# Normalised rows and the two small stacks of a fused attention and expert kernel, made by GpSimd instead of VectorE

## The reference, cut to what matters

```python
xn = layernorm(x)                                  # no gain, no bias
kv_c = xn @ W_kv;  kv_c = kv_c * rsqrt(mean(kv_c**2) + 1e-6) * g_kv     # 32 columns
q_c  = xn @ W_q                                    # 64 columns
k = concat(kv_c @ W_kdec, rope(xn @ W_krope))      # 16 heads of 8 + 32
q = concat(q_c @ W_qdec,  rope(q_c @ W_qrope));  v = kv_c @ W_vdec
att = softmax(causal(q k^T / sqrt(40))) @ v @ W_o
moe = sum over the top 2 of 8 of w_e * (silu(xn W1_e + b1_e) W2_e + b2_e) + 0.1 * shared(xn)
out = x + att + moe
```

## Time and profile before

| what | us |
|---|---|
| median of 3 runs | 778.36 |
| lowest and highest of them | 774.90, 778.86 |
| the profiled execution | 774.29 |
| its span, first to last instruction | 772.6 |
| busy in the span: TensorE | 650.1 |
| VectorE | 609.2 |
| ScalarE | 391.7 |
| GpSimd | 285.8 |
| mean granted TensorE clock | 0.946 of full |

### The profile page before, as it was taken

How to read it: one execution, slowest core, us unless ns; L and a number is a source line. 1 busy time by engine, 2 the same in 40 slices (tenths; PEclk the granted TensorE clock), 3 DMA queues, 4 the chain that set the end, 5 groups by cost and what they waited for, 6 DMA issues and landing times. The chain is left out here.

```text
span 772.6 us, 14715 instructions
## 1 busy us (share of the span) xinstructions
PE 650.1 (84%) x4646; PEld 510.9 (66%) x4646; DVE 609.2 (79%) x1632; ACT 391.7 (51%) x842; POOL 285.8 (37%) x284
## 2 busy tenths in 40 slices
PE   0557977898887899889798998888789999999995
PEld 0445756667665677667576776665558888888884
DVE  3758898878788878878888778888457777779896
ACT  1212544445453445545355445443357777777772
POOL 3322541626536254463242433233300000257574
PEclk9957999999999899999999999999989999999998
DMA  4254655466566465655444555435844778789753
GB/s 128 83 174 160 195 174 191 147 214 206 187 211 192 138 189 187 192 182 197 129 148 145 150 160 153 148 129 176 275 150 138 244 246 251 262 285 295 238 172 93
DMA packets 66135, 141.66 MB, mean 183 GB/s; under 512 B 9054, under 2 KB 34699, under 8 KB 66059
## 3 DMA queue, kind: packets, MB, share of 16 engines
q1 hardware_dynamic: 61059, 131.41, 53.2%
q0 software_dynamic: 4096, 8.40, 4.1%
q10 hardware_dynamic: 904, 0.92, 0.4%
HBM read 47.30 MB, written 29.88 MB: 100 GB/s over the span
## 5 line engine op out<-in xcount | busy, mean ns | idle before, releaser
L1042 DVE TENSOR_REDUCE mx<-bank 128x3 f32<-128x384 f32 x256 | 141.3, 552 | 66.9 <-PE bank L1497 65.4
L770 ACT ACTIVATE prob<-bank 128x384 f32<-128x384 f32 x256 | 125.1, 490 | 135.8 <-PE bank L1407 135.4
L660 POOL TENSOR_TENSOR rot<-rot,t 128x512 f32<-128x512 f32 x64 | 82.2, 1284 | 196.5 <-DVE t L1034 196.4
L1348 DVE TENSOR_TENSOR QK<-vaug,QK 128x512 fp32r<-128x512 f32 x124 | 86.4, 698 | 40.3 <-ACT QK L864 37.7
L719 POOL DMA_INDIRECT QK<-expert_outs,out_at x64 | 65.3, 1020 | 139.1 <-DMA expert_outs<-prob 120.8
L1494 PE MATMUL bank<-QK 120*128 120x256 f32 x256 | 97.2, 380 | 13.2 <-DVE mx L1042 7.1
L1404 PE MATMUL bank<-QK 122*128 122x256 f32 x256 | 90.9, 355 | 5.5 <-DMA QK<-mT 5.2
L1480 PE MATMUL bank<-ident,rot 128*120 128x128 f32 x384 | 69.4, 295 | 15.9 <-DVE mx L1042 11.5
L699 POOL DMA_INDIRECT expert_rows<-xn,place_of x64 | 67.0, 1046 | 38.6 <-PE bank L1407 28.7
L747 ACT ACTIVATE heads_high<-bank 120x384 fp32r<-120x384 f32 x96 | 47.1, 494 | 63.5 <-PE bank L1480 60.2
L1497 PE MATMUL bank<-mask_qk,identb 128*128 128x256 bf16 x256 | 75.9, 296 | 0.0
(11 more groups left out here) (229 smaller groups left out, 1436.5 us busy)
## 6 DMA issues: line engine op xcount, KB each, us to landing
QK<-heads_high SPq DMA_DIRECT2D x96, 200.0 KB
wb<-weight_parts SPq DMA_DIRECT2D x35, 512.0 KB, 4.7
QK<-heads_high SPq DMA_DIRECT2D x48, 240.0 KB
QK<-heads_low SPq DMA_DIRECT2D x48, 200.0 KB
weight_parts<-wb SPq DMA_DIRECT2D x18, 512.0 KB, 5.7
QK<-queries_high SPq DMA_DIRECT2D x32, 200.0 KB
rot<-expert_rows SPq DMA_DIRECT2D x23, 256.0 KB, 4.0
expert_outs<-prob SPq DMA_DIRECT2D x23, 256.0 KB, 4.5
```

The source lines that it names most:

```text
L660: nc.gpsimd.tensor_tensor(r[n][:, 0:H, DC:D], r[n][:, 0:H, DC:D], t2[n][:, :, :], ALU.add).then_inc(s_rot, 1)
L770: act_f(prob[:, h % P_SLOTS, :], ST_PS[h % 2][:, P:4 * P], ACT.Exp, scale=SCALE).then_inc(s_exp, 1)
L1042: V.tensor_reduce(mx[:, 0:3, h], B_PS[bank_of(k)][:, 0:3 * P].rearrange("p (a c) -> p a c", a=3), AX.X, ALU.max).then_inc(s_bfree[bank_of( ...
L1348: V.tensor_tensor(aparts[:, m % 2, 1, c, :], act[c], high, ALU.subtract).then_inc(s_alo, 1)
```

## The change

GpSimd makes the normalised rows directly behind the power of step 3, and for batch 0 ahead of the memsets of the value buffer. It makes both halves of q's stack at step 1, ahead of its second power, and the scaled keys with their stack directly behind that power. The copy to a high part becomes a multiplication by a tile of ones (`unit`). VectorE's four instructions of step 2, its copy L990 and its two of step 12 are gone. `s_small` now counts two for each batch, and its waiters wait for twice the number. Where `steps.need()` stands between two of them, GpSimd waits until the earlier one is done.

```diff
@@ gpsimd, set-up
             nc.gpsimd.tensor_tensor(rstd[:, :], rstd[:, :], mhalf[:, :], ALU.pow).then_inc(s_rstd, 1)
+            def normalised(b):
+                at = slice(b * NT, (b + 1) * NT)
+                pool.wait_ge(s_rstd, b + 1)
+                at_least(pool, s_afill, 3 * b - 2)
+                for j in range(NT):
+                    nc.gpsimd.tensor_scalar(xn[:, b * NT + j:b * NT + j + 1, :], xres[:, b * NT + j:b * NT + j + 1, :],
+                                            mv[:, j, 0:1], rstd[:, j:j + 1], ALU.subtract, ALU.mult).then_inc(s_xn, 1)
+            normalised(0)
             nc.gpsimd.memset(vflat, 0.0).then_inc(s_init, 1)
+            def stack_query(b, steps):
+                qc = smt[:, :, RKV:RKV + RQ]
+                pool.wait_ge(c_a, b * SMALL_STEPS + 7)
+                at_least(pool, s_afill, 3 * b)
+                steps.add(nc.gpsimd.tensor_tensor(qs[:, :, 0, :], qc, unit[:, 0:1].unsqueeze(1).to_broadcast([P, NT, RQ]),
+                                                  ALU.mult))
+                steps.need()
+                nc.gpsimd.tensor_tensor(qs[:, :, 1, :], qc, qs[:, :, 0, :], ALU.subtract).then_inc(s_small, 1)
+            def stack_keys(b, steps):
+                kv = smt[:, :, 0:RKV]
+                pool.wait_ge(s_rs, b + 1)
+                steps.add(nc.gpsimd.tensor_tensor(kv, kv, rs[:, :].unsqueeze(2).to_broadcast([P, NT, RKV]), ALU.mult))
+                steps.need()
+                steps.add(nc.gpsimd.tensor_tensor(ks[:, :, 0:3:2, :], kv.unsqueeze(2).to_broadcast([P, NT, 2, RKV]),
+                                                  unit[:, 0:1].unsqueeze(1).unsqueeze(1).to_broadcast([P, NT, 2, RKV]), ALU.mult))
+                steps.need()
+                nc.gpsimd.tensor_tensor(ks[:, :, 1, :], kv, ks[:, :, 0, :], ALU.subtract).then_inc(s_small, 1)
@@ gpsimd, turn
+                    if known(b + 3) and b > -3 and s == NORM_STEP:
+                        normalised(b + 3)
                     if known(b + 2) and s == SUM_STEP:
+                        stack_query(b + 2, stacks[b + 2])
                         pool.wait_ge(s_ms, b + 3)
                         nc.gpsimd.tensor_tensor(rs[:, :], rs[:, :], mhalf[:, :], ALU.pow).then_inc(s_rs, 1)
+                        stack_keys(b + 2, stacks[b + 2])
@@ vector
-            def normalised(b):
...
                 steps.add(V.tensor_tensor(sq[:, :, :], kv, kv, ALU.mult))
-                at_least(dve, s_afill, 3 * b)
-                steps.add(V.tensor_copy(qs[:, :, 0, :], qc))
                 steps.need()
...
-            def small_stacks(b, steps):
-                kv, qc = smt[:, :, 0:RKV], smt[:, :, RKV:RKV + RQ]
-                dve.wait_ge(s_rs, b + 1)
-                steps.add(V.tensor_tensor(kv, kv, rs[:, :].unsqueeze(2).to_broadcast([P, NT, RKV]), ALU.mult))
-                steps.need()
-                steps.add(V.tensor_copy(ks[:, :, 0:3:2, :], kv.unsqueeze(2).to_broadcast([P, NT, 2, RKV])))
-                steps.need()
-                steps.add(V.tensor_tensor(ks[:, :, 1, :], kv, ks[:, :, 0, :], ALU.subtract))
-                V.tensor_tensor(qs[:, :, 1, :], qc, qs[:, :, 0, :], ALU.subtract).then_inc(s_small, 1)
@@ tensor, step 3
-                            pe.wait_ge(s_small, b + 3)
+                            pe.wait_ge(s_small, 2 * (b + 3))
```

## The result

The changed kernel takes 765.87 us (median of 4 runs, 763.78 to 766.66), the kernel before beside it 776.63 (774.55 to 778.86). The ratio is 0.986, with a 95% interval of 0.982 to 0.990: 1.4% faster. The profiled execution took 766.66 us with a span of 764.9, against 772.6. The mean granted clock is 0.948, before 0.946. Some executions of the runs further down were slow as a whole: the ratios leave them out, and the profiles of `rows_only` and `before_light` are two such.

The account below looks back on a forecast made before the run. It took the first phase as bound by TensorE, except at step 3 and steps 10 to 11, where TensorE waits for VectorE. 4.4 + 4.5 - 1.0 + 1.5 + 0.5 = 9.9 us saved gave 768 us, range 755 to 786.

Parts of the forecast that it names:

- the waits: Step 3: TensorE starts on the stacks 0.34 us sooner, 4.4 us in 13 turns; bounds 8.2 and 0.
- the clock: Behind step 3: 3 of 7 half-clock stretches go, 1.5 us each, 4.5 us; bounds none and 10.5.
- the transfer of the maxima: Read at step 6: TensorE comes sooner and waits for it in few turns, 1.0 us taken back; bounds 0 and 3.
- The stacks' chain: GpSimd's six instructions for both stacks take 2.57 us plus starts, ready at 297.19, so TensorE's 0.49 us wait goes.
- The slower rival: GpSimd's small instructions cost nearly the power's price, stacks come later: 796 us, 784 at 0.6 each; chance 0.17.
- The port: Step 2: q's instructions on GpSimd hold up VectorE's L1063 by 0.3 us, net 0.15 later for what follows.
- the even rival: Both of q's instructions hold VectorE up, stacks start as late as before: 777 us; chance 0.22.
- The rows: Step 12: L975 leaves VectorE, three router turns gain 1.5 us; two GpSimd instructions of 0.4 each, bounds 0.3 to 0.85.
- The fill: Start of the pipeline: TensorE's 0.74 us wait for rows goes, first two stacks come 0.3 later each: 0.5 us gained.
- Batch 0's early rows: Start: rows come at about 6 us instead of 9.9, but VectorE waits for a transfer until 13.32: nothing gained.

Follow-up runs that it names:

- rows_only: Kernel after with both stacks put back on VectorE, only the layer norm's rows on GpSimd, against the kernel before: ratio 0.988 (0.980 to 0.996).
- before_light: Kernel before with the routed experts' split weight stores cut to 32 of 1024 columns, against the kernel before: ratio 0.999, 799.04 us.
- both: Kernel after with q's low half made behind the keys' stack and the rows' store issued later, against the kernel before: ratio 0.990.
- again: Kernel after, unchanged, run once more against the kernel before: 766.76 us, ratio 0.988.
- light_store: Kernel after with the routed experts' split weight stores cut to 32 of 1024 columns, against the kernel before: ratio 0.982.
- light_again: The same kernel as light_store, on the chip of before_light, against the kernel before: ratio 0.979, 784.35 us.
- qlow_last: Kernel after with q's low half made behind the keys' stack, against the kernel before: 765.54 us, ratio 0.986.

## Why the prediction was right, and where it was not

The forecast of 1.3% and the measured 1.4% agree. The mechanism held; the close number is in part luck: the waits and the clock gave 2.5 and 2.0 us more than forecast, the transfer of the maxima took 4.6 more, and 2.0 us were lost where the sum had nothing.

**The stacks' chain** was right. GpSimd's instructions take 0.44 and 0.46 us at q's stack and 0.29, 0.40 and 0.32 at the keys', where I took 0.40, 0.45 and 0.30, 0.40, 0.30. Ready after 2.98 us, put at 2.97 without the step to TensorE. The Trainium skill, "GPSIMD Engine Reference", section 3.1, gave the estimate 0.48 and 0.35 for the two-input kind, and these traces, with 0.46 and 0.32, lie between it and mine. The slower rival falls. The gain there is 0.53 us a turn, not 0.34: TensorE starts on L1609 0.12 us behind the start of L1520, not behind its modelled end 0.28 later. In 13 turns that is 6.9 us for 4.4, inside the bound of 8.2.

**The port** was right in size: L1081 is held up by 0.25 us (I took 0.3), and TensorE's L1494 and L1520 come 0.12 later behind VectorE's step 1 (I took 0.15). L1018, which reads two operands in SBUF, stays at 0.22, and the scaling L1022 at 0.17, so the even rival falls. But it falls by the order in time: in all 16 turns L1018 starts 0.04 us or more ahead of L679, and L1022 0.05 ahead of L682. My argument against it, that L992 and L994 read only one operand, is what spared L1020 beside L679 (0.22), not L1022. At step 10, where GpSimd starts first, a scaling is held up in the kernel after:

```profile
147.62 1.26 POOL L672 TENSOR_TENSOR rot<-rot,t 128x512 f32<-128x512 f32 x1
147.72 1.20 DVE L1085 TENSOR_SCALAR nhl<-mx 128x16 fp32r<-128x16 f32 x1
```

So L1022 stands 0.05 us on the right side. The lock of the Trainium skill, "SBUF — State Buffer", section "SBUF: two separate sides", is what L1081 shows with its 0.42 us.

**The clock.** All 7 slow stretches behind step 3 are gone, where I took 3. In no profile with the stacks on GpSimd and no added work does one stand there, nine profiles in all, while the four with the stacks on VectorE have 5 to 9. Others come elsewhere, so in these turns 11 became 7, 13.6 us less at half clock. How many come elsewhere differs from execution to execution and kernel to kernel: the nine profiles have 5 to 11 in all (the 11 in `both`), the four 11 to 15. The price was right: a least-squares fit through the 14 rows of the table gives turns = 310 + 0.99 x idle + 0.47 x time at half clock, with no residual over 1.9 us, so 3.4 us at half clock cost 1.6. Without `rows_only` and `before_light` it gives 310, 1.00 and 0.46. The term is 6.5 us, for 4.5. Behind b = 13, leaving out a last stretch that runs into the end in both, the time at half clock rose from 13.7 to 20.5 us and the rest of the program took 291.6 instead of 289.6 us: 2.0 us that my sum did not have.

**The transfer of the maxima** is the mis-sized term: 1.0 us with an upper bound of 3; measured 6.7 - 1.1 = 5.6, and 9.7 in `again`. The failed step is "up to 0.5 us in turns where the transfer is as slow as in that one. Few are". Both halves were wrong. First, the shift: I counted only the 0.34 and 0.15 us. But the slow stretch behind step 3 lies between the issue and the read, so it gave the transfer 1.5 us more. Before, in a turn with such a stretch, and then after, in a turn that waits for nothing:

```profile
166.37 0.62 ACTq L759 DMA_DIRECT2D QK<-mT  x1
...
171.29 0.36 PE L1404 MATMUL bank<-QK 122*128 122x256 f32 x1
```

```profile
417.35 0.62 ACTq L798 DMA_DIRECT2D QK<-mT  x1
...
420.11 0.36 PE L1418 MATMUL bank<-QK 122*128 122x256 f32 x1
```

The read was due 4.92 us behind the issue in turns with such a stretch and 3.40 in those without; now it is due about 2.8 behind it in all. Second, "few": of the transfers of b = 1 to 9 before, 7 landed later than 2.2 us, and a waiting read starts 0.6 us behind the landing. With those landing times, 4.14, 4.37, 3.30, 3.13, 2.29, 2.71 and 3.18, reads due at 2.77 wait 7.9 us in all. That number was to be had from the trace before, and it agrees with what the kernels after show (6.7 to 10.8). So the change took away idle time that also covered a transfer, and part of the clock's gain goes to it. Its new idle time has slow stretches of its own behind it.

**The rows.** The three router turns' waits fell from 3.5 us in all to 1.7, 1.8 less for 1.5 expected. Their instructions take 0.80 us each on GpSimd, twice my 0.40 and near the upper bound, which its idle time covers. Here are the group, and the router turn of the earlier trace rows:

```profile
L656 POOL TENSOR_SCALAR xn<-xres,mv,rstd 128x128 f32<-128x128 f32 x32 | 25.4, 796 | 1.7
```

```profile
126.79 0.41 PE L1625 MATMUL bank<-ident,xn 128*128 128x128 f32 x2 [0.75 <-DVE rank L1155]
```

The fill gave 0.2 us (the stack transposes of b = 1 at 99.17 for 99.33), not 0.5. Batch 0's early rows gave nothing, as expected: VectorE stands at L948 until 14.11 for the transfer of the earlier trace rows.

**The sum measured**, from the profiles: 9.5 us in the turns (of it idle time 54.6 - 53.2 = 1.4; clock 6.5; 1.6 unassigned), 0.2 ahead of them, 2.0 lost behind them: 7.7, which is the difference of the spans. The medians differ by 10.8. One profile can't carry more: `light_store` and `light_again`, one kernel, differ by 4.9 us in the turns, by their slow stretches. One slip in the rivals: at 0.6 us for each of GpSimd's instructions the sum gives 783, not 784.

## What to carry to other kernels

Moving a small chain to an idle engine is worth its wait plus what that wait does to TensorE's clock, here about as much as the wait (6.5 us of clock for 6.9 of waits). Before pricing a wait that goes, list every transfer that is issued ahead of it and read behind it, with its landing time in each turn: what was idle, or at half clock, was cover for it. Order the moved chain so that neither the port nor its own end is late; here each cost about 0.3 us, and exchanging the one for the other gave nothing.

## What the runs showed of the hardware

The transfer of 16 KB lands 1.7 us behind its issue in every profile from b = 10 on, and up to 5.0 us behind it (`qlow_last`) in the turns 1 to 9, in which weights are loaded, split and stored. GpSimd with two scalars by partition takes 0.80 us for 128 columns where a product by ones takes 0.44 and a subtraction 0.46. VectorE was held up beside GpSimd's subtraction of 128 columns (L1081, 0.42 us) but not beside its power of 2 columns (L1085, 0.17); nor was it when its own instruction had started 0.04 us ahead of GpSimd's (L1018, 0.22). And 0.47 us of added work on VectorE each turn, ahead of waits of TensorE, left nothing of a gain that kernels without it show as 0.9 to 1.4%.
